# A graph network's expert loop: a ring of three chunks instead of four, its first and last turn written out, and expert weights in 4 KB pieces

## What is computed

```python
x = gc + (feats @ W_res + b_res)                  # gc: the layer's graph convolution
vals, idx = jax.lax.top_k(x @ Wg + bg, 2)
gates = jax.nn.softmax(vals, axis=-1)
# for every node n and each of its two experts e, with gate g:
#   core[n] += g * (gelu(x[n] @ w1[e] + b1[e]) @ w2[e] + b2[e])      w1: 256 x 512, w2: 512 x 256, f32
y = x + core
out = (y - mean(y)) * rsqrt(var(y) + 1e-5) * gamma + beta            # over the nodes
```

## Time and profile before

| | |
|---|---|
| time, median of 3 runs | 1963.7 us (1962.0 to 1967.8) |
| the profiled execution | 1963.0 us, its span 1961.3 us |
| PE busy | 1768.7 us, 90% of the span |
| DVE, ACT, POOL busy | 949.3 (48%), 486.4 (25%), 492.8 us (25%) |
| mean over the span | 278 GB/s |
| chunks made (L688) and stored (L760) | 84 |
| rows loads (L473) | 88, of 128 KB |
| w1 and w2 loads | 176, of 512 KB |
| experts' loop | first turn at 1549.8, last chunk made at 1888.5 us |

### The profile page before, as it was taken

How to read it: one execution, slowest core, us unless ns; L and a number is a source line. 1 busy time by engine, 2 the same in 40 slices (tenths; PEclk the granted TensorE clock), 3 DMA queues, 4 the chain that set the end, 5 groups by cost and what they waited for, 6 DMA issues and landing times.

```text
span 1961.3 us, 34807 instructions
## 1 busy us (share of the span) xinstructions
PE 1768.7 (90%) x9576; PEld 1423.0 (73%) x9577; DVE 949.3 (48%) x2841; ACT 486.4 (25%) x1278; POOL 492.8 (25%) x905
## 2 busy tenths in 40 slices
PE   4888887699989999999999999999999599999961
PEld 2455555588878888788888878877777488888851
DVE  7876664444445511121221127766666734434456
ACT  0144444322223311122221111111212132233223
POOL 1122222311113300000000002217778733233314
PEclk7999998799999999999999999999999799999976
DMA  4189999899869888766658878887776499999992
GB/s 133 41 285 307 315 318 344 299 325 325 308 231 374 325 310 288 266 217 217 206 197 304 288 274 290 292 280 237 246 261 214 145 350 377 375 375 375 373 363 69
DMA packets 276800, 545.13 MB, mean 278 GB/s; under 512 B 18358, under 2 KB 201184, under 8 KB 272992
## 3 DMA queue, kind: packets, MB, share of 16 engines
q1 hardware_dynamic: 266720, 525.41, 78.6%
q0 software_dynamic: 8032, 17.63, 2.4%
q10 hardware_dynamic: 1952, 0.95, 0.3%
HBM read 415.12 MB, written 128.81 MB: 277 GB/s over the span
## 4 chain that ended last, share of the span: by engine, by line
PE 73%; DVE 11%; DMA 6%; issue 4%; DVEq 2%; SPq 1%; POOL 1%; ACT 1%; ACTq 0%; POOLq 0%
PE psum L1065 41%; PE psum L562 7%; PE psum L572 7%; PE psum L1162 4%; PE psum L957 4%; PE psum L954 3%; PE psum L976 2%; DMA blk<-counts_src_on_rows 2%; PE psum L1144 1%; PE psum L554 1%; PE psum L1173 1%; SPq L783 1%; DMA expert_weights<-expert_rows_out 1%; DMA counts_src_on_rows<-blk 1%; DMA route<-expert_rows_in 1%
## 5 line engine op out<-in xcount | busy, mean ns | idle before, releaser
L1065 PE MATMUL psum<-xsa,blk 128*128 128x512 f32 x2500 | 638.7, 403 | 11.9 <-DVE xsa L1631 9.7
L1065 PEld LDWEIGHTS psum<-xsa,blk 128*128 128x128 f32 x2500 | 456.8, 189 | 99.2 <-issue 12.6
L1065 PE MATMUL psum<-xsb,blk 128*128 128x512 f32 (+1 forms) x1875 | 407.9, 366 | 8.5 <-DMA blk<-counts_src_on_rows 5.2
L1065 PEld LDWEIGHTS psum<-xsb,blk 128*128 128x128 f32 x1875 | 316.1, 190 | 62.1 <-issue 8.6
L1904 POOL TENSOR_SCALAR ve<-mv 128x1 f32<-128x1 f32 x75 | 16.8, 224 | 763.1 <-DVE mv L1607 763.1
L1492 DVE TENSOR_SCALAR onehots<-counts_scratch 128x348 bf16<-128x348 f16 x464 | 161.6, 374 | 86.1 <-issue 45.8
L954 PE MATMUL psum<-onehots 128*128 128x349 bf16 x464 | 149.3, 322 | 38.7 <-DVE onehots L1497 38.2
L957 PE MATMUL psum<-zrow 128*128 128x512 bf16 x464 | 176.1, 389 | 0.0
L562 PE MATMUL psum<-route,expert_weights 128*128 128x128 f32 x1360 | 171.6, 281 | 4.3 <-DVE route L659 4.2
L562 PEld LDWEIGHTS psum<-route,expert_weights 128*128 128x128 f32 x1360 | 162.0, 195 | 6.1 <-DVE route L659 5.0
L572 PE MATMUL psum<-expert_weights,route 128*128 128x256 f32 x672 | 159.0, 380 | 0.0
(11 more groups left out here) (316 smaller groups left out, 2109.2 us busy)
## 6 DMA issues: line engine op xcount, KB each, us to landing
blk<-counts_src_on_rows SPq DMA_DIRECT2D x125, 832.0 KB, 5.9
blk<-counts_src_on_rows SPq DMA_DIRECT2D x125, 768.0 KB, 4.8
expert_weights<-in_L_gnn_w SPq DMA_DIRECT2D x176, 512.0 KB, 5.8
blk<-counts_dst_on_rows SPq DMA_DIRECT2D x50, 832.0 KB, 4.4
counts_dst_on_rows<-band_rows SPq DMA_DIRECT2D x25, 1600.0 KB, 8.1
blk<-counts_dst_on_rows SPq DMA_DIRECT2D x50, 768.0 KB, 4.2
counts_src_on_rows<-blk SPq DMA_DIRECT2D x13, 1600.0 KB, 8.7
counts_src_on_rows<-rblk SPq DMA_DIRECT2D x12, 1600.0 KB, 9.7
```

The costliest lines, as they stand in the source:

```text
L1065: mm = e.matmul(o, blk[n][:, k * P:(k + 1) * P], XS[:, k, :, 0:Fw], start=(k == 0), stop=(k == T - 1 and not own), skip_group_check=True)
```

## The change

- `RING` is 3. All buffers of the loop, `xTs`, `hTs` and the PSUM banks too, are three deep and indexed by n; `par` goes. The number of turns is a third of the pages, rounded up (a multiplication and a shift), and the number of the last turn stands beside it in `nturn`.
- `w1` and `w2` are read with each partition's rows next to each other in DRAM: one piece of 4 KB per partition. Partition p then holds input features 2p and 2p + 1 of w1, so the turn transposes every second column of `xin`; it holds hidden units 4p to 4p + 3 of w2, so the hidden sums take every fourth column of w1, and b1 is turned likewise.
- Turn 0 and the last turn are written out. In turn 0 the table of picks is turned behind the second matmul of chunk 0; in the last turn nothing more is loaded, turned or summed ahead. SP's loop ends one turn earlier.
- PE no longer waits for the copy of the chunk before, nor for the gelu ahead of the hidden sums; once per turn it waits for `chunk_made`.
- DVE's sum over x moves into the layer's tile loop, one add per tile; the chunks are added to the same `R2`, and the last joining add goes.

```diff
-RING = 4
+RING = 3
...
+    PART_BITS = 16
+    PART = (1 << PART_BITS) // RING + 1
...
+        turned = [psum[:, n, 0:F] for n in (0, 1, 6)]
+        summed = [psum[:, 2 + n, :] for n in range(RING)]
+        made_rows = [psum[:, 2 + RING + n, 0:F] for n in range(RING)]
...
+        def turns_of(e):
+            return e.value_load(nturn[0:1, 0:1], min_val=TOP * N // P // RING, max_val=MAXCH // RING)
+
+        def last_turn_of(e):
+            return e.value_load(nturn[0:1, 1:2], min_val=TOP * N // P // RING - 1, max_val=MAXCH // RING - 1)
...
             def load_w1(ex, n):
-                e.dma_start(w1s[n], A["L3_gnn_w1"][bass.ds(ex, 1), :, :].rearrange("a (k p) h -> p (a k) h", p=P))\
+                e.dma_start(w1s[n], A["L3_gnn_w1"][bass.ds(ex, 1), :, :].rearrange("a (p k) h -> p (a k) h", p=P))\
...
-            turns = e.value_load(nturn[0:1, 0:1], min_val=1, max_val=MAXCH // RING)
-            with e.Fori(0, turns) as j:
+            turns, ending = turns_of(e), last_turn_of(e)
+            with e.Fori(0, ending) as j:
                 for n in range(RING):
...
-                    e.wait_ge(S("chunk_made"), c + 3)
+                    e.wait_ge(S("chunk_made"), c + 1 + RING)
                     load_w2(ex, n)
...
-            def turn(c, j, n, par):
+            def turn(j, n):
                 e.wait_ge(S(f"rows_in{n}"), 16 * j + 16)
                 for k in range(KF):
-                    mm = e.transpose(psum[:, par, k * P:(k + 1) * P], xin[n][:, k * P:(k + 1) * P], identF[:, :])
+                    mm = e.transpose(turned[n][:, k * P:(k + 1) * P], xin[n].rearrange("p (c k) -> p k c", k=KF)[:, k, :], identF[:, :])
...
-                        mm = e.matmul(psum[:, 2 + par, h * P:(h + 1) * P], w1s[n][:, k, h * P:(h + 1) * P],
-                                      xTs[par][:, k * P:(k + 1) * P], start=(k == 0), stop=(k == KF - 1))
+                        mm = e.matmul(summed[n][:, h * P:(h + 1) * P], w1s[n].rearrange("p k (c h) -> p k h c", h=HT)[:, k, h, :],
+                                      xTs[n][:, k * P:(k + 1) * P], start=(k == 0), stop=(k == KF - 1))
...
-                    e.wait_ge(S("chunk_copied"), c + 1)
-                    turn(c + 2, j + (n + 2) // RING, (n + 2) % RING, par)
-
-                    e.wait_ge(S("gelu_made"), c)
-                    hidden(c + 1, j + (n + 1) // RING, (n + 1) % RING, 1 - par)
-                    rows_out(c, j, n, par)
...
+                    if not (ends and n + 2 >= RING):
+                        if n == 0 and not starts:
+
+                            e.wait_ge(S("chunk_made"), c + 2)
+                        turn(j + (n + 2) // RING, (n + 2) % RING)
+                    if not (ends and n + 1 >= RING):
+                        hidden(c + 1, j + (n + 1) // RING, (n + 1) % RING)
+                    rows_out(c, j, n)
+                    if n == 0 and starts:
+                        e.wait_ge(S("inputs_loaded"), 16 * (LOADS + 2))
+                        for a in range(2):
+                            mm = e.transpose(pids[a], pick_rows[0:NCH, :, a], identF[0:NCH, 0:NCH])
+                        mm.then_inc(S("ids_turned"), 1)
+            chunks(0, starts=True)
+            with e.Fori(1, ending) as j:
+                chunks(j)
+            chunks(ending, ends=True)
...
-            e.wait_ge(S("tile_x4_kept"), past("l3", "x4_kept") + T)
-            st.done(e.tensor_reduce(R2[:, :], X4[:, 0:T - 1, :].rearrange("p t f -> p f t"), AX.X, ALU.add))
-            st.done(e.scalar_tensor_tensor(R2[:, :], X4[:, T - 1, :], valid[:, T - 1:T], R2[:, :], ALU.mult, ALU.add))
...
-                    e.tensor_tensor(V2[:, :], V2[:, :], yout[n], ALU.add).then_inc(S("rows_added"), 1)
...
+                    e.tensor_tensor(R2[:, :], R2[:, :], yout[n], ALU.add).then_inc(S("rows_added"), 1)
...
                 e.tensor_tensor(V[:, :], pD[0], bc["gc"][:, :], ALU.add).then_inc(S("tile_x4_made"), 1)
+
+                e.wait_ge(S("tile_x4_made"), past("l3", "x4_made") + i + 1)
+                e.wait_ge(S("rows_added"), i + 1)
+                if i < T - 1:
+                    e.tensor_tensor(R2[:, :], R2[:, :], V[:, :], ALU.add).then_inc(S("rows_added"), 1)
```

More of the change, by code:

```diff
@@ L87, in gnn_program @@
     NCH = MAXCH + RING
+    PART_BITS = 16
+    PART = (1 << PART_BITS) // RING + 1
+    assert all(n * PART >> PART_BITS == n // RING and n * PART < 1 << 24 for n in range(MAXCH + RING))
     YROWS = -(-TOP * NP // (P * (T - 3)))
@@ L337, in gnn_program @@
         pdec, px4 = psum[:, 5, P:2 * P], psum[:, 5, 0:F]
+        turned = [psum[:, n, 0:F] for n in (0, 1, 6)]
+        summed = [psum[:, 2 + n, :] for n in range(RING)]
+        made_rows = [psum[:, 2 + RING + n, 0:F] for n in range(RING)]
+        pids = [psum[:, 7, a * NCH:(a + 1) * NCH] for a in range(2)]
+        assert RING == 3 and 2 * NCH <= BANK
         block = ctx.enter_context(nc.Block())
@@ L521, in sync_moe @@
                 e.wait_ge(S(f"rows_stored{n}"), 16 * turns)
-            e.wait_ge(S("gelu_made"), RING * turns + 1)
+            carry_wait(e)
+            e.wait_ge(S("gelu_made"), RING * turns)
             carry_wait(e)
@@ L585, in pe_moe, with chunks @@
+            turn(0, 0)
+            turn(0, 1)
+            hidden(0, 0, 0)
+            def chunks(j, ends=False, starts=False):
                 for n in range(RING):
                     c = RING * j + n
-                    par = n % 2
-                    e.wait_ge(S("chunk_copied"), c + 1)
-                    turn(c + 2, j + (n + 2) // RING, (n + 2) % RING, par)
-                    e.wait_ge(S("gelu_made"), c)
-                    hidden(c + 1, j + (n + 1) // RING, (n + 1) % RING, 1 - par)
@@ L598, in pe_moe @@
+            e.wait_ge(S("rows_added"), RING * turns + T + 1)
+            carry_wait(e)
+            e.matmul(psum[:, 0, 0:F], ones[:, :], R2[:, :], start=True, stop=True).then_inc(S("bn_summed"), 1)
             for g, (lo, hi) in enumerate(COMBINED):
@@ L618, in gelu, with chunks @@
                 for h in range(HT):
-                    mm = e.activation(hTs[par][:, h, :], psum[:, 2 + par, h * P:(h + 1) * P], ACT.Gelu,
+                    mm = e.activation(hTs[n][:, h, :], summed[n][:, h * P:(h + 1) * P], ACT.Gelu,
                                       bias=b1T[:, h, bass.ds(ex, 1)])
                 mm.then_inc(S("gelu_made"), 1)
-            turns = e.value_load(nturn[0:1, 0:1], min_val=1, max_val=MAXCH // RING)
+            turns, ending = turns_of(e), last_turn_of(e)
             gelu(0, 0)
-            with e.Fori(0, turns) as j:
-                for n in range(RING):
-                    c, par = RING * j + n, n % 2
+            def chunks(j, ends):
+                for n in range(RING - 1 if ends else RING):
+                    c = RING * j + n
                     e.wait_ge(S("chunk_summed"), c)
-                    gelu(c + 1, 1 - par)
+                    gelu(c + 1, (n + 1) % RING)
+            with e.Fori(0, ending) as j:
+                chunks(j, False)
+            chunks(ending, True)
             for g, (lo, hi) in enumerate(COMBINED):
@@ L685, in dve_moe @@
                     e.wait_ge(S("chunk_summed"), c + 1)
[L686 removed]
+                    if not starts:
+                        e.wait_ge(S(f"rows_stored{n}"), 16 * j)
                     carry_wait(e)
[L688 removed]
+                    e.scalar_tensor_tensor(yout[n], made_rows[n], gate_of[:, bass.ds(c, 1)], b2s[n], ALU.mult, ALU.add)\
                         .then_inc(S("chunk_made"), 1)
[L691 to L692 removed]
+                    e.wait_ge(S("rows_added"), c + T + 1)
+                    e.wait_ge(S("chunk_made"), c + 1 + RING)
                     carry_wait(e)
[L694 to L698 removed]
+                    e.tensor_tensor(R2[:, :], R2[:, :], yout[n], ALU.add).then_inc(S("rows_added"), 1)
+            chunks(0, starts=True)
+            with e.Fori(1, ending) as j:
+                chunks(j)
+            chunks(ending, ends=True)
             e.wait_ge(S("bn_summed"), 1)
```

72 lines of the change are left out of this document (35 added, 37 removed).

## The result

The changed kernel took **2123.3 us** (median of 4 runs, 2119.8 to 2132.7) against 1964.7 (4 runs, 1962.0 to 1967.8): ratio 1.081, 95% interval 1.077 to 1.085. Slower was forecast, but 2029 with a range that ended at 2085: the direction was right, the size wrong by 94 us.

A forecast was written before the change was run, and what follows sets the result against it. The prediction took the rows' landing as the loop's bound: 1566.9 + 76 x 5.0 + 9.9 = 1956.8 for the last finished chunk against 1888.5, +68.3 less 2.0 for the last store, on 1963.0: 2029 us, range 1983 to 2085.

The forecast's parts named there:

- The closed loop: Experts' loop: rows' landing sets the pace; with three buffers the period is (6.61 + L) / 2, 5.0 us against 3.85.
- Strided weight loads: Hidden matmuls' and turns' weight loads: taken as costing nothing, from L582; upper bound hidden 1.79 to 3.58 us.
- the rival: Hidden matmuls: strided loads outlasting 0.112 us double the pairs' spacing, period 5.9 us, 2097 us; chance 0.09.
- L: Rows load in the experts' loop, time from issue to landing: taken as 3.4 us, bounds 2.2 and 5.0.
- SP's step: SP's queue, from the made chunk to the issue of the next rows load: 1.94 us.
- The pieces' 0.1 us: w2 load ahead of the rows: 4 KB pieces take 1.29 us against 1.40, bringing L from 3.5 to 3.4.
- 81 chunks, last store: Experts' loop and its end: 81 chunks instead of 84; last store leaves an empty queue, -2.0 us.
- First turn: Loop's start: sum over tiles and wait for ids move away, so iteration 2 starts at 1566.9 instead of 1571.88.
- Last turn: Loop's end: no rows awaited from iteration 78 on, 9.9 us from there to the last finished chunk.
- The fast one: Experts' loop: rows land in time and the loop returns to PE's 3.75 us, 1932 us; chance 0.08.
- PE's clock: PE in the experts' loop: half clock because PE waits, period 6.9 us, 2173 us; chance 0.04.
- dummy chunks: Experts' loop: routing on the chip fills one page more, so 84 chunks run, 2044 us; chance 0.02.

The follow-up runs named there:

- experiment 1: Changed kernel with the old layouts of w1, w2, b1 and the rows' turn (no strided weight loads), ring of three kept: 2059.4 us, ratio 1.049.
- experiment 3: Changed kernel with SP's order alone changed: w1 first, then the rows of chunk c+4, ahead of the wait for the made chunk: 2084.8 us, ratio 1.060.
- Experiment 4: Changed kernel with w2 in two 2 KB pieces a partition, so w1's columns lie 8 bytes apart instead of 16: 2055.0 us, ratio 1.047.
- experiment 5: Changed kernel with the rows loaded early and hidden's weight loads taking w1 columns 32 bytes apart: 2088.4 us, ratio 1.065.
- Experiment 8: Kernel before, ring of four, with w1 in 4 KB and w2 in 2 KB pieces and 8-byte steps alone: 1972.7 us, ratio 1.003.
- experiment 7: Changed kernel, every load as early as its buffer is free: old layouts 1944.8 us; faster version, w1 4 KB, w2 2 KB pieces, 8-byte step, 1940.4 us.

## Why the prediction was right and wrong

- **The closed loop: right.** The loop before closes over the rows' landing, and three buffers take one iteration from it. In experiment 1, where PE needs 3.75 us a chunk, no period of the window is under 4.47; in the changed kernel 33 of 40 turns waited for rows. Its chain is that loop, its three parts add up to the measured period, and experiments 1 and 3 show the wait from both sides.
- **Strided weight loads: the step that failed.** "I take nothing, from L582." Hidden takes 3.72 us a chunk instead of 1.79 to 1.86, and that lies wholly on the trip from turn to made chunk: 6.66 us instead of 4.67, 1.0 us a period, 76 of the 103 us by which the profiled execution missed the forecast. The choice of row was at fault. L582 has an 8-byte step, and 8 and 16 bytes lie on different sides of an edge (experiments 4 and 5): a row at half the step was no row near it. The sign given for the rival, a load that outlasts the 0.112 us between pairs, could not tell either: the earlier trace rows has unstrided loads of 192 ns, longer than that already, and the pairs stood 0.112 apart all the same; at 329 ns they stand 0.233 apart (3.72 / 16). The bound from above, a doubled spacing, was the truth, and the sentence on the 16-byte lines pointed to it; a chance of 0.09 was far too small. The price was nearly right: the rival's mechanism held and gave 2097.
- **L: mis-sized.** Taken 3.4, measured 3.95 from issue to turn (the chain above has 4.10, and 3.13 and 4.39 one trip before and after): 0.28 us a period, 21 us. The two loads of the earlier trace rows stand at the stage's start. L did sink from the 5.0 of the full queues, but less than taken, and not in step with the DMA share: 3.91 at 0.84 in experiment 1, 3.95 at 0.72 here. What sets it the runs do not separate. SP's step was right: 1.91 against 1.94.
- **The pieces' 0.1 us: not shown.** Experiment 8 speaks against any gain for the rows where the DMA engines are full. Experiment 4, which differs from 1 in the pieces and the steps alone, has 3.64 us from issue to turn against 3.91, so a gain in emptier queues is open.
- **81 chunks, last store:** right. 81 stores stand in the page; what follows the last L717 is 70.3 us (2130.9 - 2060.6) against 72.8 before, -2.5 for a forecast of -2.0.
- **First turn: 3.3 us late.** Iteration 2 was to start at 1566.9 and started at 1570.22. Chunk 0 was made at 1564.84 instead of 1561.7: L711 took 2.20 us instead of 0.34, and PE had turned the table of picks only at 1561.21, where the forecast had it free at 1559.85. From there it is 1.82 to the rows' issue and 3.56 to the turn, where 1.83 and 3.4 were taken. That the sum per tile costs nothing holds: the first turn stands at 1550.01, before at 1549.80.
- **Last turn: 13.7 us instead of 9.9,** by two strided hiddens of 1.93 more. Experiment 1, without them, has 9.8 (1972.44 to 1982.25).
- **The sum.** 3.3 + 76 x 1.27 + 3.8 - 0.5 = 103: the forecast's 2029 plus that is 2132, and the profiled execution took 2132.7.
- **Rivals.** The fast one fell (most turns waited for rows). PE's clock hardly fell: 0.98 in the window. No dummy chunks. The range failed since its cases were priced one at a time: strided loads with an L above 3.4 were nowhere in it, and its upper end, 2085, lay below the 2097 of the rival that came true.

## What to carry to other kernels

An operand's step is a cost of its own: compare the step in bytes with a row that has the same step, and if the profile has none, let the upper bound stand with a real chance, above all where the load already fills the time between two matmuls (192 ns a load against 0.112 us a pair). When a ring loses a buffer, write down for each load how many iterations lie between issue and use; shortening one lead moves the wait to the next load (here from the rows to w1). With three buffers the order of the loads was enough to let PE run without a stop; the same order with four was not run.

## What the runs showed of the hardware

**DVE stands still beside POOL's adds.** DVE's first scaling of a bias row, 128 x 256 and 0.34 us elsewhere, took 2.20 us in the changed kernel, 4.02 in experiment 1 and 4.33 in the faster version of experiment 7. POOL's adds to X (2.87 us each) ran at that time, and each time DVE's instruction ended 0.16 to 0.17 us after the last of them: 1564.18 after 1564.02 in the changed kernel. The timeline of experiment 1:

```profile
1554.24 5.73 POOL L776 TENSOR_TENSOR X<-X,bc_bet 128x1280 f32<-128x1280 f32 x2
...
1556.12 4.02 DVE L711 TENSOR_SCALAR route<-route 128x256 f32<-128x256 f32 x1 [0.26 <-DVE route L705]
```

The kernel before shows it too, in DVE's last step of the sum over x, which ended 0.28 us after POOL's last add:

```profile
1550.19 14.33 POOL L746 TENSOR_TENSOR X<-X,bc_bet 128x1280 f32<-128x1280 f32 x5
...
1562.15 2.65 DVE L668 SCALAR_TENSOR_TENSOR R<-X,valid,R 128x256 f32<-128x256 f32 x1
```

DVE's copies out of PSUM did not stand still: in the changed kernel L704, at 1561.25 amid the adds, took 0.28 us, as its counterpart does in the run below without adds beside it.

A last run moved the adds behind POOL's loop (it is the faster version of experiment 7 in all else):

```diff
-            for g in range(T // SPLIT):
-
-                b = slice(g * SPLIT, (g + 1) * SPLIT)
-                e.tensor_tensor(X[:, b, :], X[:, b, :], bc["bet"][:, :].unsqueeze(1).to_broadcast([P, SPLIT, F]), ALU.add)
             e.wait_ge(S("picks_known"), 1)
...
+            for g in range(T // SPLIT):
+
+                b = slice(g * SPLIT, (g + 1) * SPLIT)
+                e.tensor_tensor(X[:, b, :], X[:, b, :], bc["bet"][:, :].unsqueeze(1).to_broadcast([P, SPLIT, F]), ALU.add)
             e.wait_ge(S("bn_steps"), 1)
```

> The kernel with all loads early and the 8-byte step, and POOL's five adds of the shift to X (2.87 us each) moved from ahead of its loop to behind it. In that kernel DVE's first scaling of a bias row (L717) took 4.33 us in place of 0.34 and ended 0.16 us after POOL's last add. Theory (DVE's instruction stands still while POOL's adds run): the first L717 takes 0.34 us, and from the first turn to the turn of iteration 2 go 17 us instead of 20.9. Rival (it waits for something else that the record does not name, b2's landing or the gelu's table): 4 us again, 20 to 21 us. At the end the five adds now lie beside the last load of 16 us; the whole is 1936 us if they are hidden there, up to 1950 if DVE's work there stands still in turn.

Measured: 1946.4 us, ratio 0.990 (0.988 to 0.993): no gain over the 0.987 without the move (the intervals overlap). (The turn that the expectation puts in iteration 2 is that of iteration 3, in both kernels.) Start and end in the timeline:

```profile
1545.74 0.73 PEld L577 LDWEIGHTS psum<-identF,route 128*128 128x128 f32 x4 [2.25 <-issue]
...
1556.33 0.35 DVE L717 TENSOR_SCALAR route<-route 128x256 f32<-128x256 f32 x1 [0.26 <-DVE route L711]
...
1562.89 0.41 PEld L577 LDWEIGHTS psum<-identF,route 128*128 128x128 f32 x2
```

```profile
1863.71 14.21 POOL L797 TENSOR_TENSOR X<-X,bc_bet 128x1280 f32<-128x1280 f32 x5
1863.77 21.11 DVE L739 TENSOR_TENSOR X<-X,G 128x512 f32<-128x512 f32 x5
```

The scaling takes 0.35 us and the turn comes 17.15 us after the first, as expected of the theory. At the end the same thing happens again: DVE's five subtractions stretch over 21.11 us, the first of them standing still through POOL's 14.21, and the combine of the outputs starts behind them. In experiment 7, without adds beside them, the five took a third of that:

```profile
1870.17 7.10 DVE L739 TENSOR_TENSOR X<-X,G 128x512 f32<-128x512 f32 x5
```

The Trainium skill, "SBUF — State Buffer", section "SBUF: two separate sides", states a cause: DVE and POOL share a pair of ports, and between a POOL instruction and a DVE instruction that needs the pair (one in a two-port mode, or with two inputs in SBUF) whichever starts first holds it for its whole instruction, while the other stands still. The trace agrees as to the standing still; that the ports are its cause no run here shows, and in experiment 1 DVE waited through more than one of POOL's adds.
